# A gate broadcast made once per expert instead of once per quarter, and x loaded by one queue, in a transformer layer with a dense-gated expert network

## The reference

```python
scores = jax.nn.softmax(xf @ Wg.T, axis=-1)
expert_weights, expert_indices = jax.lax.top_k(scores, K)          # K = 2 of E = 8
expert_weights = expert_weights / expert_weights.sum(-1, keepdims=True)
gates = (one_hot(expert_indices, E) * expert_weights[..., None]).sum(axis=1)
h1 = _lora_in(xf, W1, b1, A1, B1)      # 1024 -> 2048, rank 16 added
h3 = _lora_in(xf, W3, b3, A3, B3)
g = jax.nn.silu(h1) * h3
y_e = _lora_out(g, W2, b2, A2, B2)     # 2048 -> 1024, rank 16 added
y = jnp.einsum('te,ted->td', gates, y_e)
```

## Time and profile before

| | us |
|---|---|
| median of 3 runs | 7931.65 |
| lowest, highest | 7930.88, 8104.02 |
| the profiled execution, its own time | 7944.43 |
| its span on the slowest core (core 0) | 7942.9 |
| spans of the other cores | 7904.7 to 7932.3 |
| busy in it: TensorE, VectorE, ScalarE, GpSimd | 5529.2, 3300.7, 1410.1, 312.6 |

### The profile page before, as it was taken

How to read it: one execution, slowest core, us unless ns; L and a number is a source line. 1 busy time by engine, 2 the same in 40 slices (tenths; PEclk the granted TensorE clock), 3 DMA queues, 4 the chain that set the end, 5 groups by cost and what they waited for, 6 DMA issues and landing times.

```text
span 7942.9 us, 72055 instructions; the slowest of 8 cores (7904.7 to 7942.9 us)
## 1 busy us (share of the span) xinstructions
PE 5529.2 (70%) x22384; PEld 2101.6 (26%) x22384; DVE 3300.7 (42%) x6024; ACT 1410.1 (18%) x1824; POOL 312.6 (4%) x349
## 2 busy tenths in 40 slices
PE   5151133247677776328888889888889888898897
PEld 1020000013454452003223323223233233232232
DVE  2745544476666662343323323333233233333332
ACT  1012200002344341011111111111111111111111
POOL 0012200000000000000000000000000000000000
PEclk8565555566555557669879989899899899999998
DMA  3110000020000001021211212111212112121211
GB/s 93 53 11 0 0 0 0 3 50 6 1 1 1 1 1 53 0 33 17 33 17 17 33 17 33 17 26 24 28 22 30 21 17 33 17 33 17 33 17 43
DMA packets 149720, 169.27 MB, mean 21 GB/s; under 512 B 56132, under 2 KB 125268, under 8 KB 142948
## 3 DMA queue, kind: packets, MB, share of 16 engines
q0 software_dynamic: 142416, 124.21, 10.8%
q1 hardware_dynamic: 6932, 40.45, 1.5%
HBM read 267.68 MB, written 8.39 MB: 35 GB/s over the span
## 4 chain that ended last, share of the span: by engine, by line
PE 47%; DVE 4%; issue 2%; ACT 1%; DMA 1%; POOL 0%; DVEq 0%; ACTq 0%; PEldq 0%; POOLq 0%
PE pSIM L1458 24%; PE pSIM L1532 13%; PE pSIM L1463 4%; PE pMISC L1419 2%; PE pMISC L1500 2%; DVE x L1555 2%; PE pSIM L1538 1%; ACT gtmp L1482 1%; DVE gTq L1493 1%; DVE gtmp L1487 1%; DMA b3ce<-b3c 1%; DVE u2sb L1511 0%; PE pSIM L1441 0%; DVEq L179 0%; DVE u3sb L1437 0%
## 5 line engine op out<-in xcount | busy, mean ns | idle before, releaser
L1532 PE MATMUL pSIM<-gTq,w2b 128*128 128x512 bf16 x4096 | 1214.8, 444 | 308.0 <-DVE gTq L1493 225.3
L1555 DVE SCALAR_TENSOR_TENSOR x<-pSIM,x 128x512 f32<-128x512 f32 x1024 | 708.5, 692 | 790.2 <-PE pSIM L1532 452.7
L1458 PE MATMUL pSIM<-xl2T,w1b 128*128 128x512 bf16 x4096 | 986.9, 384 | 21.6 <-DVE u3sb L1437 21.6
L1487 DVE TENSOR_TENSOR gtmp<-gtmp,gtmp 128x512 bf16<-128x512 bf16 x512 | 217.7, 425 | 1859.1 <-ACT gtmp L1482 1859.1
L1458 PE MATMUL pSIM<-xl2T,w3b 128*128 128x512 bf16 x4096 | 972.8, 380 | 0.0
L1473 ACT ACTIVATE gtmp<-pSIM,b1ce 128x512 bf16<-128x512 f32 x512 | 352.1, 688 | 2952.0 <-PE pSIM L1463 2925.5
L1532 PEld LDWEIGHTS pSIM<-gTq,w2b 128*128 128x128 bf16 x4096 | 386.6, 108 | 1055.4 <-issue 871.1
L1458 PEld LDWEIGHTS pSIM<-xl2T,w1b 128*128 128x128 bf16 x4096 | 361.7, 98 | 511.8 <-issue 155.1
L1458 PEld LDWEIGHTS pSIM<-xl2T,w3b 128*128 128x128 bf16 x4096 | 358.5, 98 | 480.5 <-issue 117.7
L830 PE MATMUL pT<-idbf,lattnT 128*128 128x128 bf16 x128 | 33.9, 265 | 648.2 <-DVE lattnT L825 648.2
L1482 ACT ACTIVATE gtmp<-pSIM,b3ce 128x512 bf16<-128x512 f32 x512 | 352.0, 688 | 716.8 <-PE pSIM L1463 716.8
(11 more groups left out here) (267 smaller groups left out, 4761.5 us busy)
## 6 DMA issues: line engine op xcount, KB each, us to landing
w1b<-w1q POOLq DMA_DIRECT2D x32, 1024.0 KB, 11.6
w3b<-w3q POOLq DMA_DIRECT2D x32, 1024.0 KB, 16.8
w2b<-w2q POOLq DMA_DIRECT2D x32, 1024.0 KB, 20.1
xs<-xT SPq DMA_DIRECT2D x20, 1024.0 KB, 4.9
xc<-xT SPq DMA_DIRECT2D x8, 1024.0 KB, 5.5
xc<-xT POOLq DMA_DIRECT2D x8, 1024.0 KB, 5.6
out<-x SPq DMA_DIRECT2D x8, 1024.0 KB, 11.2
xs<-xT POOLq DMA_DIRECT2D x4, 1024.0 KB, 6.3
```

The costliest lines, as they stand in the source:

```text
L1458: E.matmul(pSIM[:, 512 * bank:512 * bank + 512], wb[:, 512 * dc + 128 * hc:512 * dc + 128 * hc + 128], xl2T[:, 2048 * dc + 512 * tc: 2048 ...
L1487: P.do("vector", lambda E: E.tensor_mul(gtmp1[:, :], gtmp1[:, :], gtmp2[:, :]), waits=[(S["scl"], S["scl"].n), (S["scl2"], S["scl2"].n), ( ...
L1532: ins = E.matmul(pch(yb), w2b[par][:, 1024 * hc + 128 * dc: 1024 * hc + 128 * dc + 128], gTq[:, 512 * hc:512 * hc + 512], start=(hc == 0), ...
L1555: E.scalar_tensor_tensor(x1[:, 2048 * dc + 512 * tc: 2048 * dc + 512 * tc + 512], pch(yb), 1.0, x1[:, 2048 * dc + 512 * tc: 2048 * dc + 51 ...
```

## The change

It does four things.

1. The gate broadcast and its copy are recorded only for q = 0. `gateb` grows from 512 to 2048 columns, one part for each tc, and the four quarters of an expert read it.
2. The wait for the adds into `x1`, which stood at the gate's matmul, moves to the two groups behind it: L1458 on `w1b` waits for all adds but the last, L1458 on `w3b` for all.
3. `xload` loses its `alt` mode: all 24 tiles of the three passes go by SP's queue, those of odd number with semaphore `sd1`.
4. The semaphore `sd2` goes.

```diff
-    gateb = sat("gateb", [128, 512], BF16, SINA + 2048)
+    gateb = sat("gateb", [128, 2048], BF16, SINA + 2048)
...
-    def xload(dst, dc, waits, alt=False):
-        if alt and dc % 2:
-            sem, eng = S["sd2"], "gpsimd"
-        else:
-            sem, eng = S[f"sd{dc % 2}"], "sync"
-        P.dma(eng, dst, xT[128 * dc:128 * dc + 128, :], waits=waits, inc=sem)
+    def xload(dst, dc, waits):
+        sem = S[f"sd{dc % 2}"]
+        P.dma("sync", dst, xT[128 * dc:128 * dc + 128, :], waits=waits, inc=sem)
         return [(sem, sem.n)]
...
-            P.do("tensor", (lambda e=e, tc=tc: lambda E:
-                            E.matmul(pch(3), sel8[:, 128 * e:128 * e + 128],
-                                     gatesF[:, 512 * tc:512 * tc + 512],
-                                     start=True, stop=True))(),
-                 waits=[(S["tev"], S["tev"].n), (S["vec2"], S["vec2"].n),
-                        (S["oe"], S["oe"].n), (S["scl2"], S["scl2"].n)],
-                 inc=S["rb"])
-            P.do("vector", lambda E: E.tensor_copy(gateb[:, :], pch(3)),
-                 waits=[(S["rb"], S["rb"].n), (S["vec"], S["vec"].n)],
-                 inc=S["tev"], drain=True)
+            if q == 0:
+                P.do("tensor", (lambda e=e, tc=tc: lambda E:
+                                E.matmul(pch(3), sel8[:, 128 * e:128 * e + 128],
+                                         gatesF[:, 512 * tc:512 * tc + 512],
+                                         start=True, stop=True))(),
+                     waits=[(S["tev"], S["tev"].n), (S["vec2"], S["vec2"].n),
+                            (S["oe"], S["oe"].n), (S["scl2"], S["scl2"].n)],
+                     inc=S["rb"])
+                P.do("vector", (lambda tc=tc: lambda E:
+                                E.tensor_copy(gateb[:, 512 * tc:512 * tc + 512],
+                                              pch(3)))(),
+                     waits=[(S["rb"], S["rb"].n), (S["vec"], S["vec"].n)],
+                     inc=S["tev"], drain=True)
             UTC = S["vec"].n
...
                 P.do("tensor", h13(w1b[par], b1tqb[par], u1sb, b1bank),
                      waits=[sg_at[eq_i], (S["vec"], UTC),
-                            (S["scl"], max(0, S["scl"].n - 1))],
+                            (S["scl"], max(0, S["scl"].n - 1)),
+                            (S["oe"], max(0, S["oe"].n - 1))],
                      inc=S["mm"])
...
                      waits=[(S["scl2"], max(0, S["scl2"].n - 1)),
-                            (S["tev"], S["tev"].n)], inc=S["sim"])
+                            (S["tev"], S["tev"].n),
+                            (S["oe"], S["oe"].n)], inc=S["sim"])
...
-                P.do("vector", (lambda hc=hc: lambda E:
+                P.do("vector", (lambda hc=hc, tc=tc: lambda E:
                                 E.tensor_mul(gTq[:, 512 * hc:512 * hc + 512],
-                                             gtmp1[:, :], gateb[:, :]))(),
+                                             gtmp1[:, :],
+                                             gateb[:, 512 * tc:512 * tc + 512]))(),
                      inc=S["vec"], drain=True)
```

More of the change, by code:

```diff
@@ L372, in pch @@
         return pSIM[:, 512 * i:512 * i + 512]
-    names = ["sd0", "sd1", "sd2", "sdc", "sgc", "sgs0", "sgs1", "sgw", "sgn", "sgf",
+    names = ["sd0", "sd1", "sdc", "sgc", "sgs0", "sgs1", "sgw", "sgn", "sgf",
              "sgp0", "sgp1", "mm", "mm2", "mm3", "mm4", "vec", "vec2", "vec3",
@@ L452, in bcast @@
              waits=[(S["mm"], S["mm"].n)], inc=S["scl"], drain=True)
-    def xload(dst, dc, waits, alt=False):
-        if alt and dc % 2:
-            sem, eng = S["sd2"], "gpsimd"
-        else:
-            sem, eng = S[f"sd{dc % 2}"], "sync"
-        P.dma(eng, dst, xT[128 * dc:128 * dc + 128, :], waits=waits, inc=sem)
+    def xload(dst, dc, waits):
+        sem = S[f"sd{dc % 2}"]
+        P.dma("sync", dst, xT[128 * dc:128 * dc + 128, :], waits=waits, inc=sem)
         return [(sem, sem.n)]
     for dc in range(8):
-        ld = xload(xch(dc)[:, :], dc, [(S["mm"], max(0, S["mm"].n - 1))],
-                   alt=True)
+        ld = xload(xch(dc)[:, :], dc, [(S["mm"], max(0, S["mm"].n - 1))])
         P.do("scalar", (lambda d=dc: lambda E:
@@ L487, in build @@
     for dc in range(8):
-        ld = xload(xch(dc)[:, :], dc, [(S["vec"], max(0, S["vec"].n - 1))],
-                   alt=True)
+        ld = xload(xch(dc)[:, :], dc, [(S["vec"], max(0, S["vec"].n - 1))])
         P.do("vector", (lambda d=dc: lambda E:
@@ L593, in build @@
     for dc in range(8):
-        ld = xload(xs2[dc % 2][:, :], dc, [(S["vec"], max(0, S["vec"].n - 4))],
-                   alt=True)
+        ld = xload(xs2[dc % 2][:, :], dc, [(S["vec"], max(0, S["vec"].n - 4))])
         P.do("vector", (lambda d=dc: lambda E:
```

## The result

| | before | after |
|---|---|---|
| median of 10 runs each, same chip | 7956.60 | 7835.09 |
| lowest, highest | 7927.91, 8139.61 | 7823.35, 7902.19 |
| the profiled execution | 7944.43 | 7823.35 |
| its spans, core by core | 7904.7 to 7942.9 | 7791.5 to 7821.8 |

The ratio is 0.986 with an interval of 0.9835 to 0.9886: 111 us less, between 91 and 131. Between the two profiled executions it is 121 us. The forecast was 72 us less and 7860; the mark of 2% was not reached. So the direction and the range held, and the size was 40 us too small.

A forecast was written before the change was run, and what follows sets the result against it. TensorE's stream in the expert stage (4419 of 7943 us) was taken as the bound. Savings 21.1 + 7.2 + 29.0 + 4.8 + 9.7 + 0 = 71.8 us gave 7860 from a median of 7931.65; range 7825 to 7890.

The forecast's parts named there:

- Only TensorE's stream counts: Last stage: only a shorter TensorE stream saves time; the 96 dropped VectorE copies, 66 us, are worth nothing.
- Kind 1: 48 blocks, q=1 and 2, tc=1 to 3: L1500 to first L1458 shrinks from 1.39 to 0.95 us; 21.1 us saved.
- Kind 2: 24 blocks opening quarters q=1 to 3 (tc=0): only the gate's slot goes, 0.30 us each; 7.2 us saved.
- that wait stays: At a quarter's start: the 1.51 us from L1500, behind the no-op counting the quarter done, remains.
- Kinds 3 and 4: Inside q=3, tc=1 to 3: 21 blocks save 1.38 us each, 29.0; the first expert's 3 save 1.60 each, 4.8.
- The loads: First three passes: 12 of 24 loads of x change queue, all covered by slack; 0, bounds 4.02 us either way.
- The clock term: Inside q=3: closing the 1.01 us gap ends seven slow first groups of L1458, 1.38 us each; 9.7 us saved.
- That gap is not touched.: The 2.33 us TensorE idle gap before a block's output, with clock falls behind it, stays; no saving counted.
- The first rival: q=1 and 2: busier TensorE spares a third of 72 blocks the fall after the 2.33 us gap; 37 us more; 22%.
- falls just move: Clock changes drift against the blocks; some 20 blocks lose 1.54 us each, 7891; part of a rival given 20%.
- The slower rival: After the 2.33 us gap, 16 matmuls run slow instead of 8 in all 128 blocks: 218 us more, 8088; 3%.
- at 3523 us within 4: Sign: the stretch before the last stage keeps its length; if it moves, the loads are the cause.

The follow-up runs named there:

- e7: Changed kernel with the next block's first w1b group issued before a block's output where the next block has q > 0, output on banks 2 and 3; ratio 0.9388.
- e9: Changed kernel with one spare 8 x 512 matmul at the head of the 96 blocks with q > 0; profiled execution 7897.07 us.
- e4: Changed kernel, but a block's first group on w1b waits for all adds into x, not all but the last; ratio 0.9903.
- e1: Kernel before with only the loads changed: all 24 loads of x on SP's queue; ratio 1.0004.
- e2: Changed kernel with the loads of x alternating between SP and POOL as before, so the gate part alone; ratio 0.9899.
- e11: Changed kernel with eight spare 8 x 512 matmuls at the head of the 96 blocks with q > 0; profiled execution 8001.17 us.

## Why the prediction was right, and where it was short

- **Only TensorE's stream counts.** Right. 66 us of VectorE went without a trace of their own: L1486, the first product, still waited 4.45 us for ScalarE in a block of the kernel after (4.08 in the earlier trace rows).
- **Kind 1**, 0.44 a block: measured 0.43 at the boundary.
- **Kind 2**, 0.30: measured 0.20, so 4.8 us, not 7.2. The start of L1455 takes 1.61 us from L1500, where the gate's had taken 1.51. The step that failed is "that wait stays": the 1.51 us were not the no-op's alone. Behind the same no-op e7 and e9 start at 1.35, so part of the time belongs to what is waited for next, and the group on w1b has one new wait more than the gate had.
- **Kinds 3 and 4**, 1.38 and 1.60: measured 1.38 and 1.60 at the boundary. The margin of 0.35 us for the last add but one held; e4 shows what it would have cost otherwise.
- **The loads**, 0: right (e1, e2), and so was the slack that was given as the cover.
- **The clock term**, 9.7 us. Its number is near: before, 50 of 168 first groups are slow, 6.25 a core or 8.6 us, after none; together with kind 3 it was to be 38.7 and came to 40.8. There is luck in that: it was read from core 0 alone, which has seven, while the others have from 2 to 12. Its reason, that the gap ahead of them makes the clock fall, is half right at most: e4 has the gap at all 168 and no fall.
- **"That gap is not touched."** True of the gap, and the wrong conclusion for its cost. The first rival had the right mechanism, fewer falls at the 2.33 us gap. I gave it 22% because few blocks were free of a fall and the gap was the same. The share went from 0.14 to 0.31 of 96 blocks, 17 blocks or so at 1.5 us, and the falls that are left became a little shorter: 27 to 30 us in all, against the 37 that it was priced at. So the step that was mis-sized is this term, which the sum put at nothing. The rival's reason, a busier TensorE, found no support: with one pad fewer blocks are free of a fall, with eight more.
- **The rival "falls just move"** was the same effect with the other sign. It was as open as the first: by the table a block 0.5 us longer or shorter decides between them, and nothing in one profile of before tells which.
- **The slower rival** (everything behind the gap slow): did not come.
- **The sum.** 71.8 forecast, 103.9 in the stage. The other 7 of the 111 us by the ratio are ahead of the stage: its first gate matmul started at 3486 to 3530 us on the eight cores of before (mean 3503), at 3486 to 3507 after (3496). The same start varied from 3484 to 3532 in e2 (old loads), and from 3487 to 3516 in e1 (new loads), whose time did not change. So I don't put it down to the loads; what it is stays open. It also means that the sign "at 3523 us within 4" was of no use: core 0 moved from 3523 to 3486, by no more than cores of one execution differ.

## What to carry to other kernels

Price an idle gap of TensorE in a dense stream at its length and at the fall of the clock behind it: here 2.33 us of idleness cost about 1.5 us more in 7 to 9 of 10 blocks of most kernels, in 4 of 10 with eight pads. That second part goes with the length of the block, so a change of half a microsecond there moved it by some 27 us over the stage, and it can go either way; put that into the range as a term of its own, and test a small gain with a pad before believing it. Rather than only shave the work beside such a gap, fill it with the next block's first group: that was worth 375 us more here (e7), over three times the whole change.

## What was not expected of the hardware

- The share of gaps behind which the clock falls is no steady function of how busy TensorE is: 28%, 16%, 11%, 25% and 60% of blocks free of it with 0, 1, 2, 4 and 8 spare matmuls of 0.2 to 0.3 us each.
- A group of 8 can run at the lower level with no idleness ahead of it, behind eight matmuls of 8 rows (3.40 us at 5652.29 in e11), and a group behind 1.01 us of idleness at the upper one, 168 times out of 168 (e4).
- Ten matmuls whose result nobody reads, in each of 128 blocks, made the kernel 203 us shorter.
- Behind the no-op at a quarter's end, TensorE's next matmul starts 1.35, 1.51 or 1.61 us from L1500 with none, one or two waits not yet covered ahead of it, and no later with 128 rows than with 8.
